# First normalisation of tiles 10, 12 and 14 by two passes of ScalarE, and the hidden transpose ahead of the query transpose

## The reference, cut to what matters

```python
def fake_quant(x, scale, zp):
    q = clip(round(x / scale + zp), 0, 255)
    return (q - zp) * scale
def layernorm(x):                       # over the last axis, eps 1e-5
    return (x - mean(x)) / sqrt(var(x) + 1e-5)
x = x + tanh(g_xattn) * matmul(fake_quant(layernorm(x)), fake_quant(ctx))
x = x + tanh(g_ffn) * layernorm(x) @ ((U * S) @ V.T).T
```

## Time and profile before

| | |
|---|---|
| Median of 3 runs | 586.47 us (586.33 to 586.63) |
| Profiled execution, its time | 587.75 us |
| Its span, first to last instruction | 585.9 us |
| TensorE (PE) busy | 568.5 us, 97% |
| VectorE (DVE) busy | 445.9 us, 76% |
| ScalarE (ACT) busy | 236.3 us, 40% |
| GpSimd (POOL) busy | 194.6 us, 33% |
| Granted TensorE clock | 1.0 throughout |
| Chain that ended last | PE 91%, DVE 3%, DMA 3%, ACT 1% |

### The profile page before, as it was taken

How to read it: one execution, slowest core, us unless ns; L and a number is a source line. 1 busy time by engine, 2 the same in 40 slices (tenths; PEclk the granted TensorE clock), 3 DMA queues, 4 the chain that set the end, 5 groups by cost and what they waited for, 6 DMA issues and landing times.

```text
span 585.9 us, 7495 instructions
## 1 busy us (share of the span) xinstructions
PE 568.5 (97%) x2688; PEld 259.5 (44%) x2688; DVE 445.9 (76%) x796; ACT 236.3 (40%) x269; POOL 194.6 (33%) x146
## 2 busy tenths in 40 slices
PE   1999999999999999999999999999999999999998
PEld 0343444444444444444444444444444444444444
DVE  6879889997179882688978799789598986889222
ACT  5889988822113413638723621202530135103200
POOL 2998750000406127846542730220044005310000
PEclk9999999999999999999999999999999999999999
DMA  8999995638928796689875263423854086403722
GB/s 279 387 387 386 331 265 136 127 93 167 277 60 213 186 254 188 202 225 390 279 159 163 57 132 66 117 82 66 222 109 143 2 177 164 125 1 69 165 55 107
DMA packets 145941, 102.73 MB, mean 175 GB/s; under 512 B 108785, under 2 KB 109041, under 8 KB 145905
## 3 DMA queue, kind: packets, MB, share of 16 engines
q1 hardware_dynamic: 136912, 84.96, 54.8%
q10 hardware_dynamic: 8992, 17.30, 9.1%
HBM read 58.99 MB, written 16.78 MB: 129 GB/s over the span
## 4 chain that ended last, share of the span: by engine, by line
PE 91%; DVE 3%; DMA 3%; ACT 1%; issue 1%; POOL 0%; SPq 0%; ACTq 0%
PE bank L616 20%; PE bank L692 19%; PE bank L661 12%; PE bank L697 9%; PE bank L755 9%; PE bank L756 9%; PE bank L760 9%; DMA v_hl<-in_ctx_dram 2%; PE bank L579 1%; DVE q L1258 1%; DVE qn L1234 1%; ACT qn L884 1%; DMA par<-in_params_dram 1%; DVE st L1203 0%; ACT u8r L863 0%
## 5 line engine op out<-in xcount | busy, mean ns | idle before, releaser
L285 POOL TENSOR_SCALAR ring<-ring,bvec 128x2048 f32<-128x2048 f32 x16 | 32.9, 2059 | 258.8 <-DVE bvec L1246 258.8
L616 PE MATMUL bank<-q,qT 128*128 128x512 f16 x512 | 117.9, 382 | 0.0
L692 PE MATMUL bank<-v_hl,xT 128*128 128x512 f16 x448 | 101.3, 379 | 0.0
L290 POOL TENSOR_TENSOR ring<-ring,corr 128x512 f32<-128x512 f32 x64 | 88.8, 1417 | 22.8 <-ACT corr L966 21.8
L755 PE MATMUL bank<-u_hl,hbuf 128*128 128x512 f16 x208 | 78.9, 379 | 0.0
L756 PE MATMUL bank<-u_hl,hbuf 128*128 128x512 f16 x208 | 78.8, 379 | 0.0
L616 PEld LDWEIGHTS bank<-q,qT 128*128 128x128 f16 x512 | 50.4, 98 | 61.4 <-issue 1.4
L279 POOL TENSOR_SCALAR q<-u8r,const 128x1024 f16<-128x1024 uint8 x52 | 66.1, 1280 | 34.5 <-ACT u8r L863 30.7
L692 PEld LDWEIGHTS bank<-v_hl,xT 128*128 128x128 f16 x448 | 43.8, 98 | 52.1
L914 ACT ACTIVATE ln<-ln,const 128x1 f32<-128x1 f32 x16 | 4.7, 293 | 141.9 <-DVE ln L1343 141.9
L1417 DVE SCALAR_TENSOR_TENSOR ring<-bank,cy,ring 128x512 f32<-128x512 f32 x63 | 46.2, 744 | 16.9 <-PE bank L760 16.9
(11 more groups left out here) (174 smaller groups left out, 781.8 us busy)
## 6 DMA issues: line engine op xcount, KB each, us to landing
out_dram<-ring SPq DMA_DIRECT2D x63, 256.0 KB, 3.4
ring<-in_x_dram SPq DMA_DIRECT2D x62, 256.0 KB, 4.4
v_hl<-in_ctx_dram SPq DMA_DIRECT2D x26, 512.0 KB, 11.5
stage<-in_ctx_dram ACTq DMA_DIRECT2D x17, 512.0 KB, 5.5
u_hl<-in_L_ffn_V_dram SPq DMA_DIRECT2D x8, 512.0 KB, 11.5
corr<-in_ctx_dram ACTq DMA_DIRECT2D x8, 512.0 KB, 6.3
stage<-in_ctx_dram SPq DMA_DIRECT2D x6, 512.0 KB, 11.4
q<-in_ctx_dram ACTq DMA_DIRECT2D x4, 512.0 KB, 10.3
```

Of the source, the lines that this page charges most:

```text
L290: nc.gpsimd.tensor_tensor(xq(t, n), xq(t, n), corr[:, n * W:(n + 1) * W], ALU.add).then_inc(x1_pre, 1)
L616: mm = nc.tensor.matmul(unit_bank(t, n)[:, :], qT_of(t)[:, k, :], q2[:, n, k, :], start=(k == 0), stop=(k == KT - 1))
L692: nc.tensor.matmul(h_bank(u)[:, :], x_home(u, g)[:, half, k % 8, :], v_hl[:, k, 0, :], start=(g == 0 and a == 0 and half == 0), stop=False)
```

## The change

- A new ScalarE function `sums1(t)` is used for tiles 10, 12 and 14 (the first of each pair, `SUM_ACT`). It makes an Identity pass over the tile that leaves the row's sum in the accumulator, scales it by -1/D to the negated mean, makes a Square pass with this as bias that leaves the sum of the squared differences, and takes the root of that times 1/D plus eps. The passes' own results go into the room of the uint8 tile and are not used.
- VectorE no longer runs `sums1` and `variance1` for these tiles. Its `quantise` makes `half_var` from the sum of squares with one more 128x1 instruction and waits for the root.
- In the loop over pairs ScalarE does hid_hi(a) ahead of op2(a+2), SP does h_transpose(a) ahead of q_transpose(a+2), and VectorE does row_correction(a+2) behind quantise(b+2) instead of behind quantise(a+2).
- For tile 10 VectorE does x1_unit(8, 2) ahead of quantise(10).

```diff
+        SUM_ACT = tuple(first_of)
...
                 if more:
                     loads(b + 2)
-                    q_transpose(a + 2)
                 h_transpose(a)
                 if more:
+                    q_transpose(a + 2)
                     q_transpose(b + 2)
...
+            def sums1(t):
+                total, squares, neg = [ln1[:, t % 2, i:i + 1] for i in range(3)]
+                for n in range(NQ):
+                    act.wait_ge(x_in[t % R][n], 16 * (t // R + 1))
+                act.wait_ge(qT_in, 16 * (t - G))
+                if first_of[t] > 0:
+                    act.wait_ge(p_done, pdone(2 * first_of[t] - 1, P7))
+                nc.scalar.activation(x_u8, xt(t), ACT.Identity, accum_out=total).then_inc(sum1_ready, 1)
+                act.wait_ge(sum1_ready, first_of[t] + 1)
+                nc.scalar.activation(neg, total, ACT.Copy, scale=-1.0 / D).then_inc(neg1_ready, 1)
+                act.wait_ge(neg1_ready, first_of[t] + 1)
+                nc.scalar.activation(x_u8, xt(t), ACT.Square, bias=neg, accum_out=squares).then_inc(var1_ready, 1)
+                act.wait_ge(var1_ready, t + 1)
+                nc.scalar.activation(ln1[:, t % 2, 3:4], squares, ACT.Sqrt, bias=C_EPS, scale=1.0 / D)\
+                    .then_inc(root1_ready, 1)
...
             column_correction(1, 3)
-            root1(10)
+            sums1(10)
             quantise(10)
...
                 if more:
-                    root1(a + 2)
+                    sums1(a + 2)
                     quantise(a + 2)
+                hid_hi(a)
+                if more:
                     op2(a + 2)
-                hid_hi(a)
                 if more:
                     root1(b + 2)
...
                 dve.wait_ge(root1_ready, t + 1)
+                if t in SUM_ACT:
+                    early(ts(half_var, ln1[:, t % 2, 1:2], -0.5 / D, -0.5 * EPS, ALU.mult, ALU.add))
                 step(nc.vector.reciprocal(y, root))
...
             x1_unit(8, 0)
-            sums1(10, 0, 2)
             x1_unit(8, 1)
-            sums1(10, 2)
-            variance1(10)
+            x1_unit(8, 2)
             quantise(10)
-            x1_unit(8, 2)
             x1_unit(8, 3)
...
                 if more:
-                    sums1(a + 2)
-                    variance1(a + 2)
                     quantise(a + 2)
-                    row_correction(a + 2)
                 hid_lo(a)
                 if more:
                     sums1(b + 2)
                     variance1(b + 2)
                     quantise(b + 2)
+                    row_correction(a + 2)
                     t4(q + 1, 0, 4)
```

More of the change, by code:

```diff
@@ L155, in gated_block_program @@
         root1_ready = sem("root1_ready")
+        sum1_ready = sem("sum1_ready")
+        neg1_ready = sem("neg1_ready")
         var2_ready = sem("var2_ready")
@@ L1208, in variance1 @@
                 mean, var, neg, _, half_var = [ln1[:, t % 2, i:i + 1] for i in range(5)]
-                dve.wait_ge(st_done, t + 1)
+                dve.wait_ge(st_done, t + 1 - sum(i < t for i in SUM_ACT))
                 nc.vector.bn_aggr(ln1[:, t % 2, 0:2], st1[:, :, :]).then_inc(var1_ready, 1)
```

## The result

| | Before | After |
|---|---|---|
| Median of 6 runs each, side by side | 586.55 us (586.33 to 587.78) | 589.57 us (588.73 to 591.22) |
| Ratio, with 95% interval | | 1.0044 (1.0033 to 1.0056) |
| Profiled execution: span | 585.9 us | 588.4 us |
| VectorE (DVE) busy | 445.9 us | 442.6 us |
| ScalarE (ACT) busy | 236.3 us | 248.6 us |

The medians differ by 3.0 us.

A forecast was written before the change was run, and what follows sets the result against it. TensorE was taken to bound the kernel. 0.45 us for tile 10 plus 2 x 1.3 for the pairs made 3.05 us, on a median of 586.47: 589.5 us. Its own range was 587.9 to 591.4, widened to 586.5 to 591.4.

The forecast's parts named there:

- TensorE bounds, nothing to win: From 320 us on, TensorE is the limit; shortening other engines' work gains at most about 1.5 us.
- Part 1: Tile 10: ScalarE's passes delay root2(8) and x_hi(8), P6 of the first quad 0.45 us late (0.1 to 0.9).
- Part 2: Tiles 12 and 14 on ScalarE: quantise(12) 0.5 us late, hid_lo(10) 1.4 us earlier, no cost in the sum.
- Part 3: Moved row_correction puts GpSimd's work on VectorE's t4 and t1; 1.3 us per pair (0 to 2.0).
- rival A: No collision: shared port bandwidth or other moments for pre_row make row_correction's move free; 586.9 us; chance 0.22.
- The second meeting: Tile 13's GpSimd work meets t1 of quad 3: 1.25 us less 0.9 idle, 0.3 us lost at y_unit(11, 0).
- Pair 2: Loop turn in which tile 14 is normalised: 1.3 us lost, the loop being the same as for tile 12.
- pair 1: Loop turn in which tile 12 is normalised: 1.3 us lost.
- first meeting: Tile 12's GpSimd work meets t4 and t1: 1.0 us lost by P6 of quad 2, 0.3 at y_unit(10, 0) included.
- The signs that it named: Trace marks for right or wrong, such as P6 of the first quad 0.3 to 0.6 us late, t4 6 us or more.
- Rival B: Not slower: tile 10's delay absorbed, y_unit(a-1, 0) or P6 sooner through earlier hid_lo; 585.9 us; chance 0.08.
- Rival C: Tile 8's transposes also late, mm3(8) waits, collisions at their bound of 2.0 us a pair; 591.5 us; chance 0.10.

The follow-up runs named there:

- 1: Also tile10_only: the kernel before, with only tile 10 normalised by ScalarE's two passes and x1_unit(8, 2) ahead; ratio to before 1.0004.
- 3: Also row_back: the kernel after, with row_correction(a+2) right behind hid_lo(a), ahead of sums1(b+2); ratio to before 0.9997.
- 4: The kernel after, with GpSimd's pre_row and four pre of tiles 12 and 14 cut to 8 columns; ratio to before 1.0000.
- 5: The kernel after, with the loop's three orders (op2, q_transpose, row_correction) as before and the sums still on ScalarE; ratio to before 0.9997.
- q_first: The kernel after, with op2(a+2) again ahead of hid_hi(a) and q_transpose(a+2) ahead of h_transpose(a), row_correction left late; ratio to before 1.0072.
- 2: Also row_only: the kernel before, with only row_correction(a+2) moved behind quantise(b+2); ratio to before 1.0072.
- row_later: The kernel after, with row_correction(a+2) one step further back, behind t4; ratio to before 1.0041.
- narrow_second: The kernel after, with GpSimd's instructions for tiles 13 and 15 cut to 8 columns; ratio to before 1.0012.

## Why the prediction was right, point by point

The time was forecast as 589.5 us on a median of 586.47, a loss of 3.05; it is 589.57 on 586.55, a loss of 3.0, by the trace 2.66 and by the ratio 2.6. The direction and the mechanism hold, and the place in the loop over pairs. The parts of the sum do not all have the sizes that they were given.

- **TensorE bounds, nothing to win** holds: no variant came below the kernel before beyond its interval, among them four that keep some or all of the sums on ScalarE and lose nothing (1, 3, 4, 5). Waits at the y units are there in all, 1.4 us or more (2.8 in q_first).
- **Part 1, 0.45 us for tile 10: wrong, 0.** The mechanism was right (late root2(8), two idle pieces that absorb), the size was not. quantise(10) was 2.5 late, not 2.7. Then x_lo_half(8, 0) met less of GpSimd's work: it took 2.11 us where it had taken 2.49, so that VectorE stood 1.6 late ahead of the two idle pieces of 1.76 in place of 2.2. The term "0.45" came from a difference of large numbers, and its lower bound, 0.1, did not reach the 0 that was measured.
- **Part 2, ScalarE: no cost of its own** holds (experiment 5). quantise(12) started at 419.58, 0.3 late rather than 0.5, hid_lo(10) at 422.19 rather than 422.7.
- **Part 3, GpSimd's work falls on t4 and t1** holds, shown from three sides: moving row_correction alone costs as much and more (2), moving it back or making GpSimd's instructions short takes the cost away (3, 4). The sizes: t4 took 5.25 us, not 6.65, since its first two instructions both ran before pre_row, where the sum let them alternate from the first (pre_row's record is 2.78 long, not 1.97). y_unit(10, 0) came at 437.03, 1.6 late rather than 2.2, and TensorE's mm4(10) lost nothing there (0.3 forecast). P6 of quad 2 lost 0.34, not 1.0. The range took 0.65 a pair as its lower end, which no row gave; its other figure, 0, belonged to rival A. The pairs cost 1.1 and 1.5.
- **The second meeting, tile 13's work with t1 of quad 3: forecast 0.3, measured 0.80.** t1 was stretched by 1.07, near the 1.25 of the prediction. But I looked only at y_unit(11, 0), beyond VectorE's idle time of 0.9. TensorE waits sooner: P4 of quad 2 for the add of P7 that stands behind t1 (0.55 lost), and P6 of quad 3 for the add of P1 (0.25); in pair 2 the same two places lose 0.54 and 0.26. Those adds come ahead of the idle time, which therefore absorbed none of it.
- **Pair 2 costs 1.5, not the same as pair 1.** All of the difference is in the first meeting: P6 of quad 4 lost 0.72 instead of 0.34. sums1(15) waited 0.75 us for its load. t4 then took 2.49 us, VectorE idled for 3.26 ahead of hid_lo(13), and GpSimd's work fell on t1, as VectorE's timeline of the kernel after shows:

```profile
492.29 0.69 DVE L1223 BATCH_NORM_STATS2 st<-ring 128x6 f32<-128x512 f32 x1 [0.75 <-DMA ring<-in_x_dram]
...
500.59 0.69 DVE L1411 SCALAR_TENSOR_TENSOR hbuf<-bank,hbuf 128x512 f16<-128x512 f32 x1 [3.26 <-ACT hbuf L966]
501.19 2.76 DVE L1316 TENSOR_TENSOR xT<-q,stage 128x1024 f16<-128x1024 f16 x2
...
504.54 1.70 DVE L1316 TENSOR_TENSOR xT<-q,stage 128x1024 f16<-128x1024 f16 x2
```

- So two errors, 0.45 too much for tile 10 and 0.66 too much at the first meeting of pair 1, stand against 0.5 too little at the second, and 0.2 too little for pair 2. That the total came so close is in part luck.
- **The signs that it named.** Two of those for "right" did not come: P6 of the first quad 0.3 to 0.6 late (0), and t4 at 6 us or more (5.25, and 2.49 at tile 14). The others did, with y_unit(10, 0) 1.6 late for about 2. A t4 of 4.3 us or less was to speak for rival A; at tile 14 it did not, because the work fell on t1.
- **Rival A (shared bandwidth, or no collision)** falls by the single instructions shown above and by experiments 2 and 4. Its other half, that pre_row may get in at other moments, came true at tiles 12 and 14 and did not make the move free. **Rival B** falls: P6 and the y units came no sooner in any variant. **Rival C**: the transposes of tile 8 did not hold up mm3(8), which started at 343.75, 0.15 earlier, as the whole execution.

What makes pair 2 dearer was not tested by itself. The load of tile 15 has a part: in row_only and q_first, where sums1(15) does not wait for it, the first meetings of the two pairs cost the same (1.15 and 1.13; 1.45 and 1.45), and in row_later, with a wait of 0.54 us, they cost 0.16 and 0.80. It is not the whole: narrow_second has a wait of 0.81 us and loses 0.29 and 0.31. There two of t4's instructions ran before pre_row and not four, as VectorE's timeline of that kernel shows:

```profile
494.00 5.25 DVE L1331 TENSOR_TENSOR xs<-q,stage 128x1024 f16<-128x1024 f16 x4
499.70 0.69 DVE L1413 SCALAR_TENSOR_TENSOR hbuf<-bank,hbuf 128x512 f16<-128x512 f32 x1 [0.45 <-ACT hbuf L968]
```

So the order in which the two engines get their turns seems to count as well. With one trace of each kernel the two cannot be told apart.

## What to carry to other kernels

When an instruction is moved that releases another engine's work, place that engine's work on the time axis and look at what runs beside it: here a 0.2 us row_correction, moved by 4 to 5 us, moved 7 us of GpSimd work from beside bn_stats and the start of t4 to beside t4 and t1, at 0.7% of the kernel when done alone. Idle time absorbs a delay only for the waits that come after it, so follow each consumer in order, not just the last one. With TensorE at 97%, relieving VectorE of 9 us was worth nothing (experiment 5), and so was getting the hidden transpose sooner (experiment 3).

## What the hardware showed that I had not expected

The two engines do not strictly alternate. At tile 12 two of VectorE's instructions ran before pre_row did, and at tile 14 all four of t4: they took 2.49 us, their bare length, while pre_row's record grew to 4.07 (VectorE's and GpSimd's timelines of the kernel after).

```profile
494.83 2.49 DVE L1329 TENSOR_TENSOR xs<-q,stage 128x1024 f16<-128x1024 f16 x4
...
495.09 4.07 POOL L288 TENSOR_SCALAR ring<-ring,bvec 128x2048 f32<-128x2048 f32 x1 [44.36 <-DVE bvec L1268]
```

Its bare 1.97 us, counted back from its end at 499.16, begin at 497.2, when t4 is done. Who gets its turn when both have work ready is not settled by these runs. And bn_stats beside GpSimd's work keeps its length: sums1(13) takes 2.46 us in row_back from 422.84 on, with GpSimd at work from 423.10, and sums1(11) takes 2.46 in the kernel after, with GpSimd idle.
